# Making the scores of a whole group of heads in one piece, in eleven of sixteen groups

## The chip, the cores and the metric

The kernel runs on one core of a Trainium2 chip. The metric is the device time of one execution in microseconds (us), of which the median of several runs is taken. Engines are named as in the profile: PE is TensorE's matmul stream, DVE VectorE, ACT ScalarE, POOL GpSimd, SP the queue of SyncE.

## The reference, cut to what matters

```python
def attention(xn, ctx, mask, wq, wk, wv, wo):        # 32 sequences of 64 tokens, 512 wide
    q = rope((xn @ wq) in 32 heads of 128)
    k = rope((ctx @ wk) in 8 heads of 128, each used by 4 query heads)
    v = (ctx @ wv) in 8 heads of 128, likewise
    p = softmax(q @ k.T / sqrt(128) + mask)           # 64 x 64 per sequence and head
    return (p @ v) @ wo
x = x + tanh(g_xattn) * attention(layernorm(x), ctx, ctx, mask, ...)
x = x + tanh(g_ffn) * lora_top1_experts(layernorm(x))
```

Everything is float32. Most products are made as three products of split operands (high and low parts); the scores alone are float32 products without a split.

## The kernel before

**Stages.** Up to about 205 us the kernel makes the keys and values of all sequences. Then come 64 attention steps, `k = 0..63`, from about 216 us to the end; the last four (`WIDE = 60` and on) are written out by hand, together with the end of the experts. Four steps make a group of heads `G = k // 4`: one key head with its four query heads, over half of the sequences (16 of them, in two chunks of 8 sequences, each chunk in two steps of 4). Groups 0 to 7 are the first half of the sequences, groups 8 to 15 the second. In the first half the query weights (`weights_of`) and output weights are also split and stored beside the steps, until step 25; in the second half they are fetched ready.

**One step `k` on PE** (loop at L1065): the scores that are due; `times_values(k-1)`, probabilities times values, into the banks `attn[0]` and then `attn[1]`; two query products of the next group (each 6 matmuls, L892); `project_out(k-1, 0)` (12 matmuls, L963); in even steps a third product; `turn_probs(k)` (4 transposes, L923); `project_out(k-1, 1)`; and a last product (`last`). The query blocks are made by a seven-product scheme: blocks `b` of two heads, products numbered 0 to 6, and from them four sums `j` (`q_sum`, `SUMS`), each of which then gets its rotary embedding: DVE multiplies by the cosine (`q_cos`, L1197), ACT copies the halves crosswise (`q_shift`, L1605 and L1606), POOL multiplies by the sine (`by_sin`, L1885), DVE adds (`q_add`, L1202). Product 6, and the sum `j = 3` that needs it, end the making of a block.

**Scores.** `scores(k)` is 32 matmul instructions of 128 rows by 64 columns (L912) into bank `score` or `small`. Steps in `PAIRED` (2 to 29 and 36 to 59) make them two by two at the head of every even step, so a group has two such places. `scores` waits for the rotary adds of its queries, for its keys, and for `masked`, the mask add that last read its bank.

**Softmax of step k.** DVE adds the mask out of the bank (L1263) and finds the maximum (L1268), POOL subtracts (L1892), ACT takes the exponential (L1635), DVE sums and inverts (L1272, L1274), POOL multiplies (L1897), PE transposes, ACT copies the high part (`prob_high`, L1643, L1646), DVE makes the low part (`prob_low`, L1284).

**What PE waits for around the values.** `times_values(k)` needs both low parts of step k before its first matmul. Its second half, into `attn[1]`, also needs `x1_added` to have reached `2k`, which means that `add_out(k-1, 1)` (DVE, L1304) has read what `project_out(k-1, 1)` left in that bank:

```python
e.wait_ge(probs_low, 2 * k + 2)
...
e.wait_ge(x1_added, 2 * k - 1 + bp)
```

The order on every engine is written out by hand, and each engine runs its instructions in that order.

Of the kernel before, what the change touches and what calls it, by code (L numbers as in the profile page):

```python
# [36 lines left out]
UNITS = GROUPS * CHUNKS  # L37
# [4 lines left out]
SCALE = float(np.float32(1) / np.sqrt(np.float32(DH)))  # L42
SPLIT_PRODUCTS = ((0, 0), (0, 1), (1, 0))
TWIN_ROWS = (slice(0, SEQ), slice(SEQ, 2 * SEQ))

RAW = 2
WO_SLOTS = GROUP + 2
# [132 lines left out]
def ropes_of(k):  # L180

    early, late = sums_of(k)
    pending = sums_of(k - 1)[1] if k else [(1, 3)]
    pending = [q for q in pending if q[1] == 3]
    rest = [q for q in late if q[1] != 3]
    if len(early) == 2:
        return early[:1], early[1:], rest
    return pending, early, rest
# [116 lines left out]
def build(nc, x, ctx, mask, g_attn, g_ffn, wq, wk, wv, wo, routed_w, lora_b, table, out):  # L305
# [8 lines left out]
    with ExitStack() as stack:  # L314
# [263 lines left out]
        def _(e):  # L578
# [199 lines left out]
            for k in range(STEPS + 1):  # L778
                for j in range(k):
                    for n in wo_late(j) if wo_low_step(j) == k - 1 else ():  # L780
                        store_wo(n)
                done = KT + sum(len(wo_late(j)) for j in range(k) if wo_low_step(j) < k)
                while ring < min(len(RING), RAW + done):
                    fetch_raw(ring)
                    ring += 1
                for b, piece in weights_of(k):
                    if piece == 1 and k and b + 1 < HEAD_PAIRS_ALL:
                        fetch_wq_raw(b + 1)
                    if piece == 3:
                        store_wq(b)  # L790
                if k % 2 == 0 and HEAD_PAIRS_ALL <= k // 2 + 3 < Q_BLOCKS:
                    fetch_wq(k // 2 + 3)
                if k in (27, 28):
                    for i in {27: range(4), 28: range(4, BLOCKS)}[k]:
                        fetch_xB(i)
                if k % 2 == 1 and k // 2 + 2 < UNITS:
                    fetch_keys(k // 2 + 2)
                if k % 2 == 0 and k and k // 2 + 1 < UNITS:
                    fetch_values(k // 2 + 1)
                if k % 4 == 0:  # L800
                    G = k // 4
                    for n in range(max(GROUP * G + 2, HEADS), min(GROUP * G + 6, GROUP * GROUPS)):
                        fetch_wo(n)
                if k in (30, 32):
                    fetch_mask(CHUNKS + (k - 30) // 2)
                for t in range(HALF_TILES):
                    if 30 + t // 2 == k - 1:
                        store(t)
# [7 lines left out]
        def _(e):  # L816
# [248 lines left out]
            for k in range(1, WIDE):  # L1065
                first, middle, last = products_of(k)
                if k in PAIRED:
                    for j in (k, k + 1) if k % 2 == 0 else ():
                        scores(j)
                elif k > 1:  # L1070
                    scores(k)
                between(k, 0)
                times_values(k - 1)
                between(k, 1)
                for b, i in first[:1]:
                    product(b, i)
                between(k, 2)
                for b, i in first[1:]:
                    product(b, i)
                between(k, 3)  # L1080
                project_out(k - 1, 0)
                between(k, 4)
                for b, i in middle:
                    product(b, i)
                turn_probs(k)
                between(k, 5)
                project_out(k - 1, 1)
                between(k, 6)
                for b, i in last[:1]:
                    product(b, i)  # L1090
                between(k, 7)
                for b, i in last[1:]:
                    product(b, i)
                between(k, 8)

            k = WIDE
# [59 lines left out]
        def _(e):  # L1156
# [93 lines left out]
            def by_row(k):  # L1250
                return prob_of(k)[:, :].rearrange("p (r k) -> p r k", r=ROWS)

            def mask_scores(k, tiles=()):
                u, s = divmod(k, SUBS)
                G, c, index = chunk_of(u)
                m = mask_sb[:, c, s * SUB_SEQS:(s + 1) * SUB_SEQS, :].rearrange("p b k -> p (b k)").unsqueeze(1).to_broadcast(
                    [P, HEAD_PAIRS, SUB_SEQS * SEQ])
                e.wait_ge(scored, k + 1)
                e.wait_ge(mask_in[c], 16 * (index // CHUNKS + 1))
                if k >= 2:  # L1260
                    e.wait_ge(probs_turned, k - 1)
                by_head = prob_of(k)[:, :].rearrange("p (h n) -> p h n", h=HEAD_PAIRS)
                e.scalar_tensor_tensor(out=by_head, in0=scores_bank(k)[:, :].rearrange("p (h n) -> p h n", h=HEAD_PAIRS),  # L1263
                                       scalar=SCALE, in1=m, op0=ALU.mult, op1=ALU.add).then_inc(masked, 1)

                expert_norms_end(tiles)
                e.wait_ge(masked, k + 1)
                e.tensor_reduce(neg_max[:, k % 2, :], by_row(k), AX.X, ALU.max, negate=True).then_inc(max_found, 1)  # L1268

            def sum_rows(k):  # L1270
                e.wait_ge(exponentials, k + 1)
# [151 lines left out]
            for k in range(1, WIDE):  # L1423
                early, late = sums_of(k)
                ropes = ropes_of(k)
                mask_scores(k, norms_of(k - 1))
                attn_low(k - 1, 0)
                attn_low(k - 1, 1)
                between(k, 0)
                between(k, 1)  # L1430
                if k % 4 != 1 and k > 2:
# [4 lines left out]
                    for n in wo_late(k - 1):  # L1436
                        raw_low(("wo", n))

                for q in sums_of(k - 1)[1] + early:
                    q_sum(*q)  # L1440

                for q in (ropes_of(0)[0], ropes_of(1)[0])[k - 1] if k <= 2 else ():
                    q_cos(*q)
                    q_add(*q)
                if k > 2:
                    ropes_left(k - 1)
                between(k, 2)
                add_out(k - 1, 0)
# [9 lines left out]
                between(k, 5)  # L1458
                between(k, 6)
                prob_low(k, *((0, 1) if together else (1,)))  # L1460
                add_out(k - 1, 1)
                if k <= 2:
                    ropes_left(k - 1)
# [358 lines left out]
        def _(e):  # L1822
# [107 lines left out]
            for k in range(1, WIDE):  # L1930
                ropes = ropes_of(k)
                pieces = weights_of(k)
                subtract_max(k)
                if k == 1:
                    for q in ropes_of(0)[0]:
                        by_sin(ROPE_NO["q", *q])
                elif k == 2:
                    weight_low(*weights_of(1)[1])
                elif k % 2 == 0 and pieces:
                    combine_weights(pieces[0][0], (0,))  # L1940
                elif k % 4 == 1:
                    for n in wo_late(k - 1):
                        raw_low(("wo", n))
                elif pieces:
                    weight_low(*(pieces[0] if k > 3 else weights_of(2)[0]))
# [4 lines left out]
                if k == 1:  # L1950
# [2 lines left out]
                    for q in ropes_of(0)[1]:  # L1953
                        by_sin(ROPE_NO["q", *q])
                    combine_weights(HEAD_PAIRS + 1, (1,))
                if k % 2 == 0 and pieces:
                    combine_weights(pieces[0][0], (1,) if k > 2 else (0, 1))
                for q in ropes[0]:
                    by_sin(ROPE_NO["q", *q])
# [7 lines left out]
                    weight_low(*pieces[0 if k % 4 == 1 else 1])  # L1967
                if k % 2 == 0 and k > 2 and pieces:

                    e.wait_ge(rope_added, ROPE_NO["q", *ropes[0][0]] + 1)  # L1970
                    weight_low(*pieces[0])
                for q in ropes[1] + ropes[2]:
                    by_sin(ROPE_NO["q", *q])
# [80 lines left out]
```

## Time and profile before

| | us |
|---|---|
| median of 3 runs (1054.49 to 1057.78) | 1055.28 |
| time of the profiled execution | 1054.43 |
| its span | 1052.6 |
| PE busy | 1043.5 (99%) |
| DVE busy | 871.8 (83%) |
| ACT busy | 634.2 (60%) |
| POOL busy | 592.0 (56%) |

The profile comes from one execution. Busy times are of the span of 1052.6 us; its own run took 1.8 us more. Times in rows are us from the span's start. A merged row of the timeline gives the start of its first instruction, the time to the modelled end of the last, and the count. Matmuls overlap, so what a stretch of matmuls takes is read from its start to the start of the next row.

### The profile page before, as it was taken

The numbers are of one execution on the slowest core, as the hardware profiler recorded it, in microseconds if no ns is written. First come the engines' busy times: TensorE is split into PE (matmuls) and PEld (weight loads), VectorE is DVE, ScalarE is ACT, GpSimd is POOL, SyncE is SP. The second block draws the span as 40 slices with busy tenths as digits, with TensorE's granted clock in tenths as the row PEclk, the third lists the DMA queues.
The fourth block names the chain that finished last, engine by engine and source line by source line (L and its number), as shares of the span: only waits on it lengthen the run. The fifth ranks groups of instructions, "written<-read, shape, count | busy, mean of one in ns | idle before, by whom it ended". The sixth has DMA issues, their size and how long they took to land.

```text
span 1052.6 us, 19130 instructions
## 1 busy us (share of the span) xinstructions
PE 1043.5 (99%) x6664; PEld 865.2 (82%) x6664; DVE 871.8 (83%) x1423; ACT 634.2 (60%) x1112; POOL 592.0 (56%) x518
## 2 busy tenths in 40 slices
PE   9999999999999999999999999999999999999998
PEld 7888888877788888888888888888888888888786
DVE  7875766788888888888887999888788788888997
ACT  7554456676766676767666645555555555555653
POOL 4552379887878787878764433333443334444423
PEclk9999999999999999999999999999999999999999
DMA  7768966476765656566469745563546464644102
GB/s 262 269 226 302 395 232 240 160 282 211 249 219 182 218 183 208 192 191 210 150 246 398 247 150 171 160 198 119 201 124 201 127 197 121 194 121 134 46 26 81
DMA packets 106094, 206.40 MB, mean 196 GB/s; under 512 B 8848, under 2 KB 58640, under 8 KB 100112
## 3 DMA queue, kind: packets, MB, share of 16 engines
q1 hardware_dynamic: 105424, 204.40, 57.3%
q8 instruction: 55, 0.90, 0.4%
q10 hardware_dynamic: 576, 0.79, 0.2%
q14 instruction: 39, 0.32, 0.1%
HBM read 122.31 MB, written 82.84 MB: 195 GB/s over the span
## 4 chain that ended last, share of the span: by engine, by line
PE 91%; DVE 5%; POOL 2%; issue 1%; ACT 1%; DMA 0%; DVEq 0%; SPq 0%; ACTq 0%
PE attn L963 31%; PE proj L892 27%; PE attn L854 8%; PE score L854 4%; PE turned L854 4%; PE attn L948 3%; PE score L912 3%; PE turned L923 3%; PE attn L950 3%; PE small L912 2%; PE proj L826 1%; DVE acc L1304 1%; DVE stats L1162 1%; DVE o_s L1292 0%; DVE p_low L1284 0%
## 5 line engine op out<-in xcount | busy, mean ns | idle before, releaser
L963 PE MATMUL attn<-wo_s,o_s 128*128 128x512 f32 x1524 | 375.1, 395 | 0.6 <-DVE o_s L1292 0.5
L892 PE MATMUL proj<-xB,wq_s 128*128 128x512 f32 x1344 | 332.7, 390 | 0.0
L963 PEld LDWEIGHTS attn<-wo_s,o_s 128*128 128x128 f32 x1524 | 280.7, 188 | 58.3 <-DVE o_s L1292 1.4
L892 PEld LDWEIGHTS proj<-xB,wq_s 128*128 128x128 f32 x1344 | 251.8, 188 | 51.8 <-issue 0.4
L1885 POOL TENSOR_TENSOR rot<-rot,tab 128x512 f32<-128x512 f32 x110 | 163.3, 1485 | 146.7 <-ACT rot L1606 146.6
L1655 ACT ACTIVATE o_s<-attn 128x512 fp32r<-128x512 f32 x127 | 69.2, 596 | 89.0 <-PE attn L950 88.8
L1197 DVE TENSOR_TENSOR q_r<-q_r,tab 128x512 f32<-128x512 f32 x127 | 116.5, 918 | 1.5 <-ACT x_third L1606 1.4
L1292 DVE TENSOR_TENSOR o_s<-attn,o_s 128x512 fp32r<-128x512 f32 x127 | 81.9, 685 | 32.3 <-ACT o_s L1655 32.3
L1627 ACT ACTIVATE copies<-proj 128x512 f32<-128x512 f32 x96 | 57.5, 599 | 76.9 <-PE proj L892 76.6
L1304 DVE SCALAR_TENSOR_TENSOR acc<-attn,gates_t,acc 128x512 f32<-128x512 f32 x127 | 94.9, 748 | 6.8 <-PE attn L963 3.8
L1885 POOL TENSOR_TENSOR rot_third<-rot_third,tab 128x512 f32<-128x512 f32 x40 | 61.7, 1542 | 58.3 <-ACT rot_third L1606 55.4
L1284 DVE TENSOR_TENSOR p_low<-turned,p_high 64x512 fp32r<-64x512 f32 x128 | 87.8, 686 | 5.2 <-ACT p_high L1643 2.8
L1643 ACT ACTIVATE p_high<-turned 64x512 fp32r<-64x512 f32 x128 | 75.5, 590 | 26.2 <-PE turned L923 24.4
L1605 ACT ACTIVATE rot<-q_r 64x512 f32<-64x512 f32 x84 | 52.4, 623 | 53.1 <-DVE q_r L1241 51.3
L1646 ACT ACTIVATE p_high<-p_high 64x512 fp32r<-64x512 f32 x128 | 80.8, 631 | 2.8
L1241 DVE TENSOR_TENSOR q_r<-copies,proj 128x512 f32<-128x512 f32 x127 | 81.1, 678 | 0.3 <-PE proj L892 0.3
L1202 DVE TENSOR_TENSOR q_r<-q_r,rot 128x512 f32<-128x512 f32 x85 | 69.2, 814 | 6.0 <-POOL rot L1885 0.3
L1897 POOL TENSOR_TENSOR prob_even<-prob_even,row_inv 128x512 f32<-128x512 f32 x32 | 34.1, 1065 | 60.5 <-DVE row_inv L1274 60.5
L1897 POOL TENSOR_TENSOR prob_odd<-prob_odd,row_inv 128x512 f32<-128x512 f32 x32 | 35.8, 1117 | 39.1 <-DVE row_inv L1274 39.1
L948 PE MATMUL attn<-p_high,v_s 128*128 128x256 f32 x254 | 55.0, 298 | 2.1 <-issue 0.7
L1831 POOL TENSOR_TENSOR rstd<-var_eps,power 128x1 f32<-128x1 f32 x32 | 18.5, 578 | 68.1 <-DVE var_eps L1166 68.1
L1892 POOL TENSOR_TENSOR prob_even<-prob_even,neg_max 128x512 f32<-128x512 f32 x32 | 33.4, 1044 | 38.8 <-DVE neg_max L1268 38.8
(272 smaller groups left out, 1733.4 us busy)
## 6 DMA issues: line engine op xcount, KB each, us to landing
wq_kept<-wq_s SPq DMA_DIRECT2D x16, 1792.0 KB, 6.3
wq_s<-wq_kept SPq DMA_DIRECT2D x16, 1792.0 KB, 8.8
v_kept<-vst SPq DMA_DIRECT2D x64, 256.0 KB, 4.3
v_s<-v_kept SPq DMA_DIRECT2D x128, 128.0 KB, 4.8
wo_kept<-wo_s SPq DMA_DIRECT2D x32, 512.0 KB, 6.0
wo_s<-wo_kept SPq DMA_DIRECT2D x32, 512.0 KB, 5.4
k_kept<-kst SPq DMA_DIRECT2D x32, 256.0 KB, 2.1
wq_raw<-in_wq SPq DMA_DIRECT2D x16, 512.0 KB, 7.7
```

What stands on the lines that cost most here:

```text
L854: last = e.matmul(b[:, :], stationary, moving, start=(kt == 0 and m == 0), stop=(kt == KT - 1 and m == 2))
L892: last = e.matmul(dst[:, :], wq_s[:, b % 2, A, s, kt, :], xB[:, B, mv, kt, :], start=(first and kt == 0 and m == 0), stop=(kt == 1 and m = ...
L948: e.matmul(b[:, cols[twin]], v_s[:, u % 2, twin, tiles[bp], :], p_high[:, twin, cols[bp]], start=(twin == 0), stop=False, skip_group_check ...
L963: last = e.matmul(out_bank(k, bp)[:, :], o_s[:, s, bp, h, :], wo_s[n % WO_SLOTS][:, m, :], start=(h == 0 and i == 0), stop=(h == GROUP - 1 ...
L1197: e.tensor_tensor(dst, src, cos, ALU.mult).then_inc(times_cos, 1)
L1241: e.tensor_tensor(q_tile(b, j) if dst is None else dst, by_seq(copies[:, copy, :]), by_seq(proj[PRODUCTS[i][2]][:, :]), ALU.add).then_inc( ...
L1284: e.tensor_tensor(p_low[rows, :, twin, :], turned[rows, :].rearrange("p (b n) -> p b n", b=PAIRS), p_high[rows, twin, :].bitcast(F32).rear ...
L1292: e.tensor_tensor(low, src, high.bitcast(F32), ALU.subtract).then_inc(out_low, 1)
L1304: e.scalar_tensor_tensor(out=acc[:, tile, :], in0=out_bank(k, bp)[:, :], scalar=gates_t[:, 0:1], in1=acc[:, tile, :], op0=ALU.mult, op1=AL ...
L1643: e.activation(p_high[rows, twin, :], turned[rows, :], ACT.Copy).then_inc(probs_high, 1)
L1646: last = e.activation(p_high[TWIN_ROWS[1 - twin], twin, :], p_high[rows, twin, :].bitcast(F32), ACT.Copy)
L1885: e.tensor_tensor(r3, r3, sin, ALU.mult).then_inc(times_sin, 1)
```

## The change

`QUADS` names eleven groups, 2 to 6 and 9 to 14. In them all four `scores` of the group are made at its first step, behind query products 0 and 1 and ahead of `project_out(k-1, 0)`; the pair at the head of the group's first step and the one at the head of its third step go. Since the last two of the four need the queries of the second chunk, product 6 of the last step of the group before is made ahead of `project_out(k-1, 1)` instead of behind it, its sum and the cosine of sum 2 go ahead of `add_out(k-1, 1)` on DVE, and the remaining rotary work goes to the head of the first step. DVE adds the masks of two steps there (`add_mask`) and finds their maxima apart (`find_max`). On POOL the combining of weights goes ahead of the first step's subtraction; on SP the keys are fetched in other steps. The diff:

```diff
+QUADS = (*range(2, 7), *range(9, 15))
+def in_quad(k):
+    return k // 4 in QUADS
+def quad_begins(k):
+    return k % 4 == 0 and in_quad(k)
...
@@ ropes_of
-    pending = [q for q in pending if q[1] == 3]
-    rest = [q for q in late if q[1] != 3]
+    pending = [q for q in pending if q[1] == 3 and not quad_begins(k)]
+    rest = [q for q in late if q[1] != 3 or quad_begins(k + 1)]
...
@@ SP
-                if k % 2 == 1 and k // 2 + 2 < UNITS:
+                if k % 4 == 2 and quad_begins(k + 2):
+                    fetch_keys(k // 2 + 2)
+                elif k % 2 == 1 and k // 2 + 2 < UNITS and not quad_begins(k + 1):
                     fetch_keys(k // 2 + 2)
...
@@ PE
-                    for j in (k, k + 1) if k % 2 == 0 else ():
+                    for j in (k, k + 1) if k % 2 == 0 and not in_quad(k) else ():
                         scores(j)
...
                 for b, i in first[1:]:
                     product(b, i)
+                if quad_begins(k):
+                    for j in range(k, k + 4):
+                        scores(j)
                 between(k, 3)
                 project_out(k - 1, 0)
...
                 turn_probs(k)
                 between(k, 5)
+                for b, i in last[:1] if quad_begins(k + 1) else ():
+                    product(b, i)
                 project_out(k - 1, 1)
                 between(k, 6)
-                for b, i in last[:1]:
+                for b, i in last[:1] if not quad_begins(k + 1) else ():
                     product(b, i)
...
@@ DVE (mask_scores is split into add_mask and find_max)
-                mask_scores(k, norms_of(k - 1))
-                attn_low(k - 1, 0)
-                attn_low(k - 1, 1)
+                if quad_begins(k):
+                    second, third = ropes_of(k - 1)[1] + ropes_of(k - 1)[2]
+                    q_add(*second)
+                    q_cos(*third)
+                    attn_low(k - 1, 0)
+                    q_add(*third)
+                    add_mask(k)
+                    add_mask(k + 1)
+                    find_max(k)
+                    attn_low(k - 1, 1)
+                else:
+                    if k % 4 == 1 and in_quad(k):
+                        find_max(k)
+                    else:
+                        mask_scores(k, norms_of(k - 1))
+                    attn_low(k - 1, 0)
+                    attn_low(k - 1, 1)
...
-                for q in sums_of(k - 1)[1] + early:
+                for q in early if quad_begins(k) else sums_of(k - 1)[1] + early:
                     q_sum(*q)
...
-                if k > 2:
+                if k > 2 and not quad_begins(k):
                     ropes_left(k - 1)
...
                 prob_low(k, *((0, 1) if together else (1,)))
+                if quad_begins(k + 1):
+                    q_sum(*late[0])
+                    q_cos(*ropes[1][0])
                 add_out(k - 1, 1)
...
@@ POOL
+                if quad_begins(k) and pieces:
+                    combine_weights(pieces[0][0])
                 subtract_max(k)
...
                 elif k % 2 == 0 and pieces:
-                    combine_weights(pieces[0][0], (0,))
+                    if not quad_begins(k):
+                        combine_weights(pieces[0][0], (0,))
...
-                if k % 2 == 0 and pieces:
+                if k % 2 == 0 and pieces and not quad_begins(k):
                     combine_weights(pieces[0][0], (1,) if k > 2 else (0, 1))
...
-                    e.wait_ge(rope_added, ROPE_NO["q", *ropes[0][0]] + 1)
+                    if ropes[0]:
+                        e.wait_ge(rope_added, ROPE_NO["q", *ropes[0][0]] + 1)
```

## Rows read from the trace of the kernel before

**Rows 1.** Busy time by stretch: PE, PEld, DVE, ACT, POOL, granted clock, DMA share, GB/s

```profile
306.99:561.99 255.00, 255.00 (x1741) 212.51 (x1740) 225.08 (x328) 174.47 (x307) 195.36 (x168) 1.00 0.62 210
683.34:989.34 306.00, 306.00 (x2090) 255.01 (x2089) 247.59 (x384) 175.56 (x300) 124.07 (x97) 1.00 0.48 149
```

**Rows 2.** The list of waits, PE on DVE's output add: total, times, longest

```profile
PE attn L948 <- DVE acc L1304: 0.5, 1, 0.5
```

**Rows 3.** PE's timeline, step 23 and the head of step 24: start, us, instruction

```profile
499.95 0.40 PE L948 MATMUL attn<-p_high,v_s 128*128 128x256 f32 x2
...
500.41 0.40 PE L948 MATMUL attn<-p_high,v_s 128*128 128x256 f32 x2
...
500.89 2.90 PE L892 MATMUL proj<-xB,wq_s 128*128 128x512 f32 x12
503.63 2.88 PE L963 MATMUL attn<-wo_s,o_s 128*128 128x512 f32 x12
...
509.54 1.52 PE L892 MATMUL proj<-xB,wq_s 128*128 128x512 f32 x6
510.99 1.15 PE L912 MATMUL score<-k_r,q_r 128*64 128x64 f32 x32
...
513.01 0.50 PE L948 MATMUL attn<-p_high,v_s 128*128 128x256 f32 x2
...
513.58 0.40 PE L948 MATMUL attn<-p_high,v_s 128*128 128x256 f32 x2
```

**Rows 4.** Timeline at the kernel's end: scores alone, and a wait for the output add

```profile
989.34 1.15 PE L912 MATMUL score<-k_r,q_r 128*64 128x64 f32 x32
990.42 0.50 PE L948 MATMUL attn<-p_high,v_s 128*128 128x256 f32 x2
...
1002.05 0.50 PE L948 MATMUL attn<-p_high,v_s 128*128 128x256 f32 x2 [0.55 <-DVE acc L1304]
```
```profile
1001.25 0.75 DVE L1304 SCALAR_TENSOR_TENSOR acc<-attn,gates_t,acc 128x512 f32<-128x512 f32 x1
```

**Rows 5.** DVE's timeline, head and end of step 23 (first half)

```profile
499.38 0.75 DVE L1304 SCALAR_TENSOR_TENSOR acc<-attn,gates_t,acc 128x512 f32<-128x512 f32 x1
...
508.96 1.60 DVE L1202 TENSOR_TENSOR q_r<-q_r,rot 128x512 f32<-128x512 f32 x1
510.48 1.40 DVE L1284 TENSOR_TENSOR p_low<-turned,p_high 64x512 fp32r<-64x512 f32 x2
511.91 0.75 DVE L1304 SCALAR_TENSOR_TENSOR acc<-attn,gates_t,acc 128x512 f32<-128x512 f32 x1
```

**Rows 6.** The page's groups of DVE: cosine products and query sums

```profile
L1197 DVE TENSOR_TENSOR q_r<-q_r,tab 128x512 f32<-128x512 f32 x127 | 116.5, 918 | 1.5 <-ACT x_third L1606 1.4
...
L1241 DVE TENSOR_TENSOR q_r<-copies,proj 128x512 f32<-128x512 f32 x127 | 81.1, 678 | 0.3 <-PE proj L892 0.3
```

**Rows 7.** The timelines of DVE and PE, end of step 21 (first half)

```profile
485.66 0.69 DVE L1284 TENSOR_TENSOR p_low<-turned,p_high 64x512 fp32r<-64x512 f32 x1
486.39 0.75 DVE L1304 SCALAR_TENSOR_TENSOR acc<-attn,gates_t,acc 128x512 f32<-128x512 f32 x1
```
```profile
487.51 0.50 PE L948 MATMUL attn<-p_high,v_s 128*128 128x256 f32 x2
```

**Rows 8.** The timelines of PE, DVE, ACT and POOL, step 47 (second half)

```profile
825.29 0.40 PE L948 MATMUL attn<-p_high,v_s 128*128 128x256 f32 x2
...
831.70 0.60 PE L923 MATMUL turned<-tab,prob_odd 128*128 128x128 f32 x4
```
```profile
831.90 0.75 DVE L1304 SCALAR_TENSOR_TENSOR acc<-attn,gates_t,acc 128x512 f32<-128x512 f32 x1 [0.22 <-PE attn L963]
...
834.08 1.40 DVE L1284 TENSOR_TENSOR p_low<-turned,p_high 64x512 fp32r<-64x512 f32 x2
```
```profile
835.38 0.63 ACT L1606 ACTIVATE rot_third<-q_r 64x512 f32<-64x512 f32 x1
```
```profile
836.09 1.27 POOL L1885 TENSOR_TENSOR rot_third<-rot_third,tab 128x512 f32<-128x512 f32 x1 [3.27 <-ACT rot_third L1606]
```

More of the change, by code:

```diff
@@ L1251, in by_row, with add_mask @@
                 return prob_of(k)[:, :].rearrange("p (r k) -> p r k", r=ROWS)
-            def mask_scores(k, tiles=()):
+            def add_mask(k):
                 u, s = divmod(k, SUBS)
@@ L1264, in mask_scores, with find_max @@
                                        scalar=SCALE, in1=m, op0=ALU.mult, op1=ALU.add).then_inc(masked, 1)
-                expert_norms_end(tiles)
+            def find_max(k):
                 e.wait_ge(masked, k + 1)
                 e.tensor_reduce(neg_max[:, k % 2, :], by_row(k), AX.X, ALU.max, negate=True).then_inc(max_found, 1)
+            def mask_scores(k, tiles=()):
+                add_mask(k)
+                expert_norms_end(tiles)
+                find_max(k)
             def sum_rows(k):
@@ L1425, in _ @@
                 ropes = ropes_of(k)
-                mask_scores(k, norms_of(k - 1))
-                attn_low(k - 1, 0)
-                attn_low(k - 1, 1)
+                if quad_begins(k):
[4 more added lines that the diff above has]
+                    q_add(*third)
+                    add_mask(k)
+                    add_mask(k + 1)
[3 more added lines that the diff above has]
+                    if k % 4 == 1 and in_quad(k):
+                        find_max(k)
+                    else:
+                        mask_scores(k, norms_of(k - 1))
+                    attn_low(k - 1, 0)
+                    attn_low(k - 1, 1)
                 between(k, 0)
```

## The prediction, made before the changed kernel had run

> **What bounds the kernel now.** I read the busy times by stretch first, then PE's list of waits, then the timelines of single steps. In both halves of the attention PE is busy for every microsecond of the stretch at full clock, and DVE for 225 of 255 us in the first half but 248 of 306 in the second [rows 1]. PE's waits are nearly nothing, and only once, at the kernel's end, does it wait for the output add [rows 2]. So the order in which PE issues matmuls sets the time, and what can be gained is only what PE itself loses between them. What can be lost is slack: how long before PE needs something the other engines have it. The first-half steps must be read apart from the second-half ones, since DVE (88% busy against 81%) has less room there.
>
> **What goes: eleven entries into the scores.** The cost of one is read around the pair ahead of step 24 [rows 3]. Going in: the six matmuls of a product take 1.45 us up to the scores (509.54 to 510.99), where twelve undisturbed ones take 2.74 (500.89 to 503.63), so six take 1.37: 0.08 lost. Inside: 64 score instructions take 2.02 us (510.99 to 513.01), and 32 alone take 1.08 (989.34 to 990.42) [rows 4], so 32 more cost 0.94 and a place costs 1.08 - 0.94 = 0.14 beyond its instructions. Going out: the first half of the values takes 0.57 us (513.01 to 513.58) against 0.46 (499.95 to 500.41): 0.11. Sum 0.33; with the times unrounded I take 0.35. The eleven changed groups have two places each and get one. The new place is left into `project_out`, which the trace shows no dearer, so the gain is 11 x 0.35 = **3.9 us**. The bound from below is 11 x 0.25 if leaving into wider matmuls costs another 0.1. No matmul is added or dropped.
>
> **What is added (1): the turn of the group.** Product 6 (1.37 us) changes places with `project_out(k-1, 1)`, and the pair of scores (2.02) goes from behind it. These 3.4 us lay between `project_out(k-1, 1)` and `times_values(k)`, and were the cover for `add_out(k-1, 1)`. Now the values follow at once, and their second half needs that add. The trace lets me time every part. PE's last `project_out` matmul is followed at 831.70 by the transposes and DVE's add begins at 831.90: 0.20 us [rows 8]. The add takes 0.75, and PE goes on 0.05 after it (1002.00 to 1002.05) [rows 4]. The first half of the values covers 0.46 [rows 3]. So PE must stop for 0.20 + 0.75 + 0.05 - 0.46 = **0.54 us** at each of eleven turns, even if DVE is idle. This alone is 5.9 us against the gain of 3.9.
>
> DVE is not idle. Ahead of the add the change queues a `q_sum` (0.60 of pitch, its 0.68 [rows 6] less the 0.08 by which such instructions overlap) and a `q_cos`. In the second half the low parts end at 835.48 and a sum would end by 836.1; the `q_cos` waits for ACT's shift, as late now as before, which ends 10.72 into the step (836.01 - 825.29) [rows 8]. A `q_cos` that meets no POOL work takes 0.69, the mean of all is 0.92 [rows 6]. With 0.69 the add runs from 11.36 to 12.11 and PE's second half starts at 12.16. A step without scores is 510.99 - 499.95 = 11.04, less the 0.08 of going in: 10.96 [rows 3], so it would have started at 11.42. The stop is **0.74** at each of the six second-half turns: 4.4 us.
>
> In the first half the low parts of step 23 end at 511.88, which is 11.93 into the step, and DVE had run without a break before them (the add of the sine part ends at 510.56, the low parts start at 510.48) [rows 5]. Sum, cosine and add behind them take 0.60 + 0.60 + 0.67: the add ends at 13.80, PE's second half starts at 13.85 instead of 11.42: a stop of 2.4 us at the turn into group 2. At the four later turns PE has already come 0.6 us closer to DVE (next part) while DVE itself gains 0.3, so I take 2.65. Five turns: 2.4 + 4 x 2.65 = **13.0 us**.
>
> **What is added (2): the middle of the group.** At step 4G+2 the pair of scores vanishes ahead of `times_values(4G+1)`, and with it 2.02 + 0.08 = 2.10 us of cover. In the first half the low part of step 21 ends at 486.35, 1.16 before the values start at 487.51, and the add at 487.14, 0.83 before the second half at 487.97 to 488.08 [rows 7]. The values would start at 485.41 and their second half at 485.87; the add is ready for PE at 487.19. Stop: **1.3 us**, five times: 6.6. The change takes one mask add from DVE in that step, but DVE stands idle there anyway before it waits for ACT, so I credit nothing. In the next step DVE's slack is 0.28 (add ends at 500.13 [rows 5], second half starts at 500.41 [rows 3]) and PE is 0.9 ahead of its old time, DVE 0.35: a stop of 0.35, four times: 1.4. In the second half the low parts of the corresponding steps are ready some 3 us ahead, and 2.1 less does not hurt: step 47 as the nearest case has them at 10.19 of 10.96 [rows 8]. Nothing.
>
> **What is added (3): four scores in a row.** The third shares its bank with the first, so it waits for `add_mask(k)`. That has 0.20 + 0.69 + 0.05 = 0.94 us and the second scores take 0.94 [rows 4]; I take 0.05 at each place, 0.5 in all, and 0 to 0.2 as the bounds. It also waits for the rotary add of sum 3. In the second half its shift ends about 12.1, the sine product about 14, the add about 15.5 into the count above, and the third scores would start at 17.6. In the first half PE's own stop gives that chain more time. It is covered; every microsecond by which it were later than 2 us would cost 11. The softmax of the first step has 6.9 us from the second scores' end to the transposes, and needs about 6.1 (two DVE passes and the small inverse, two on POOL at 1.04, one on ACT); 0.8 is left. If that cover went, each 0.1 costs 1.1. Edits with one answer: the weight combining moves into POOL time that is free while PE makes scores; SP's key fetches wait for scores that are made earlier than before, and come at least one step ahead of use. Both at nothing; a late key fetch would stop PE by the lateness.
>
> **The sum.** Stops 4.4 + 13.0 + 6.6 + 1.4 + 0.5 = 25.9, gain 3.9: **+22.0 us**. The profiled execution took 1054.43, of which 1.8 lie around the span and stay: 1076.4. The median of the runs is 0.85 above it, so I forecast **1077** for the median. For the spread I let each first-half stop be off by a quarter (5 us) and `q_cos` take its mean: 1069 to 1084.
>
> **Rivals.** (a) *DVE catches up.* The work that leaves the later steps lets DVE reach the values in time in the first half, and only the eleven turns stop PE. For it: DVE has 30 us of idle time per 255 in the first half [rows 1]. Against it: its idle time lies ahead of what it waits for from ACT, not in the run before the low parts. Price: 11 x 0.74 + 0.5 - 3.9 = +4.7, 1060.
> (b) *Faster.* The turn is hidden too, and the place's cost is all that counts: 1055.28 - 3.9 = 1051. This decides where the stop at a turn is under 0.35 us; the bound of 0.54 is above that, so the bound would have to be wrong, for example if the wait for `add_out` fell on work that had ended.
> (c) *POOL takes the turn from DVE.* `q_cos(2)` on DVE and the sine product of the same sum on POOL are both released by one ACT shift. POOL's product takes 1.27 us alone, starting 0.08 after the shift [rows 8]. If it holds DVE off, the cosine ends about 1.2 later, and so do add and values: up to 11 x 1.2 = 13 more, 1090. Against it: DVE starts 0.03 to 0.05 after ACT, POOL 0.08. The Trainium skill (SBUF — State Buffer, "SBUF: two separate sides") says that the two share a port pair as an exclusive lock, and whoever starts first holds it for the whole instruction; by that rule this case is all or nothing, decided by those few hundredths. The 0.81 to 1.12 us that some cosine products take beside POOL speak for such holding off.
> (d) *Not what it says.* The third scores wait on queries that come late, so the four fall into two pieces; it costs what the chain is late, and I count it with (c).
>
> **How the numbers follow.** Forecast 0.70, (a) 0.12, (b) 0.04, (c) and (d) 0.14. The range takes in the forecast's own spread and reaches towards (a) and (c): 1065 to 1086. A difference of 0.3% (3.2 us) is what a measurement of this kernel tells from none. Faster by more is (b) alone: 0.04. Within it lies half of (a) with small turns: 0.08. Slower: 0.88.
>
> **What would show it.** After the change PE's list of waits should have about 11 entries of the second half of the values (L948) behind DVE's output add (L1304), 0.7 us each in the second half and 2 to 3 us in the first, and five to nine entries in the middle of first-half groups. The score places should fall by eleven, each at 3.9 us. The prediction is wrong if PE stays as full in the first half as now, if DVE's add at a turn ends within 0.8 us of `project_out`, or if the stops lie at the scores or at the transposes instead.

## The result and the profile after

The changed kernel takes 1095.31 us (median of 4 runs, 1091.34 to 1096.69) against 1055.31: a ratio of 1.0366, 95% interval 1.0338 to 1.0395. It is 40 us slower; the forecast was 22 us slower, with a range that ended at 1086. The profiled execution took 1096.69 us, 42.3 more than the one of before, and this is what the accounts below are made against. One execution of the kernel before (1994 us, granted clock 0.88) and one of the kernel with filled stops (1515 us, 0.66) ran in a slow state and are left out of every median and ratio below.

PE's list of waits in the changed kernel (total, times, longest). L962 is the first matmul of each half of `times_values`, L948 before; L1328 is DVE's output add, L1304 before. Before, the second line of this list read 0.5 us, once [rows 2]:

```profile
PE attn L962 <- DVE acc L1328: 17.2, 12, 1.8
PE attn L962 <- issue: 9.9, 11, 1.1
...
PE proj L906 <- issue: 0.6, 1, 0.6
```

The eleven turns and the middles of first-half groups are there, as forecast. The first line is the second half of the values, at the eleven turns and once at the kernel's end. The second is the low parts, at the five first-half turns, in the five first-half middles, and once ahead of the changed groups. What is not in this list is in the table of stretches (busy time of PE, PEld, DVE, ACT, POOL, granted clock, DMA share, GB/s), the turn into group 2 and one of the second half:

```profile
310.00:315.00 5.00, 4.27 (x13) 3.46 (x14) 4.65 (x6) 3.02 (x6) 4.21 (x3) 0.66 0.34 143
820.00:825.00 5.00, 5.00 (x49) 3.90 (x50) 1.62 (x3) 0.83 (x2) 0.00 (x0) 0.71 0.56 163
```

The granted clock (the value ahead of the DMA share) is 0.66 and 0.71: TensorE ran for part of these stretches at 1.2 instead of 2.4 GHz. Before, it was 1.00 in every stretch [rows 1].

**A second-half turn**, step 47 into 48, the timeline of PE, then of DVE, ACT and POOL. The same places before are in [rows 8]:

```profile
868.35 2.88 PE L977 MATMUL attn<-wo_s,o_s 128*128 128x512 f32 x12
871.07 0.40 PE L962 MATMUL attn<-p_high,v_s 128*128 128x256 f32 x2
871.30 0.39 PE L964 MATMUL attn<-p_low,v_both 128*128 128x512 f32 x1
873.46 0.50 PE L962 MATMUL attn<-p_high,v_s 128*128 128x256 f32 x2 [1.76 <-DVE acc L1328]
873.80 0.39 PE L964 MATMUL attn<-p_low,v_both 128*128 128x512 f32 x1
874.03 2.92 PE L906 MATMUL proj<-xB,wq_s 128*128 128x512 f32 x12
876.88 1.15 PE L926 MATMUL score<-k_r,q_r 128*64 128x64 f32 x32
877.86 1.10 PE L926 MATMUL small<-k_r,q_r 128*64 128x64 f32 x32
879.02 1.15 PE L926 MATMUL score<-k_r,q_r 128*64 128x64 f32 x32
...
881.04 1.20 PE L977 MATMUL attn<-wo_s,o_s 128*128 128x512 f32 x4
```
```profile
868.90 1.40 DVE L1308 TENSOR_TENSOR p_low<-turned,p_high 64x512 fp32r<-64x512 f32 x2
870.34 0.69 DVE L1260 TENSOR_TENSOR q_r<-copies,proj 128x512 f32<-128x512 f32 x1
870.95 1.79 DVE L1216 TENSOR_TENSOR q_r<-q_r,tab 128x512 f32<-128x512 f32 x1
872.66 0.74 DVE L1328 SCALAR_TENSOR_TENSOR acc<-attn,gates_t,acc 128x512 f32<-128x512 f32 x1
...
878.08 0.69 DVE L1282 SCALAR_TENSOR_TENSOR prob_even<-score,mask_sb 128x512 f32<-128x512 f32 x1 [1.85 <-PE score L926]
```
```profile
870.20 0.63 ACT L1647 ACTIVATE rot_third<-q_r 64x512 f32<-64x512 f32 x1
```
```profile
870.91 1.28 POOL L1926 TENSOR_TENSOR rot_third<-rot_third,tab 128x512 f32<-128x512 f32 x1 [3.27 <-ACT rot_third L1647]
```

The second half of the values would have started at 871.07 + 0.46 = 871.53 and starts at 873.46: a stop of 1.92 us (the row's 1.76 counts from the modelled end of the matmul ahead). The cosine took 1.79 us where 0.69 was forecast. POOL's sine product had started at 870.91, 0.04 before it, and took its own 1.28. Five of the six second-half turns are like this (POOL ahead by 0.02 to 0.04, cosine 1.79 to 1.81); at the first POOL is ahead by 0.41, the cosine takes 1.42 and the stop is 1.90. The four scores take 881.04 - 876.88 = 4.16 us: the third begins 1.16 after the second, where 0.93 is the pace. After the stop PE starts 0.11 slower (0.34 instead of 0.23 for the first pair of matmuls).

**A first-half turn**, step 19 into 20, timelines of PE and DVE:

```profile
474.09 2.88 PE L977 MATMUL attn<-wo_s,o_s 128*128 128x512 f32 x12
478.05 0.47 PE L962 MATMUL attn<-p_high,v_s 128*128 128x256 f32 x2 [1.07 <-issue]
...
479.98 0.50 PE L962 MATMUL attn<-p_high,v_s 128*128 128x256 f32 x2 [1.23 <-DVE acc L1328]
```
```profile
476.55 1.40 DVE L1308 TENSOR_TENSOR p_low<-turned,p_high 64x512 fp32r<-64x512 f32 x2
477.97 0.69 DVE L1260 TENSOR_TENSOR q_r<-copies,proj 128x512 f32<-128x512 f32 x1
478.58 0.69 DVE L1216 TENSOR_TENSOR q_r<-q_r,tab 128x512 f32<-128x512 f32 x1
479.18 0.74 DVE L1328 SCALAR_TENSOR_TENSOR acc<-attn,gates_t,acc 128x512 f32<-128x512 f32 x1
```

`project_out` ends at 474.09 + 2.72 = 476.81, PE stops 1.23 us for the low parts and, 0.46 after it goes on, 1.47 more for the add: 2.70. "Issue" stands at the first stop because the profile names no releaser; the low parts end at 477.95 and PE starts 0.10 later. The cosine takes 0.69: POOL's product of 476.65 ended at 477.92, and its next starts at 480.04.

**A first-half middle**, step 18, PE's timeline:

```profile
450.52 1.52 PE L906 MATMUL proj<-xB,wq_s 128*128 128x512 f32 x6
452.82 0.47 PE L962 MATMUL attn<-p_high,v_s 128*128 128x256 f32 x2 [0.78 <-issue]
...
453.56 0.51 PE L962 MATMUL attn<-p_high,v_s 128*128 128x256 f32 x2
```

The six matmuls would be done at 450.52 + 1.37 = 451.89, so PE stops 0.93 for the low parts. The second half starts 0.74 after the first instead of 0.46. Together that is 1.21.

### The profile page after: what moved, and what is told of

It is laid out like the page before. It is cut to its first block, busy times and chain, and to the rows that moved or that the text cites. A ratio compares the mean times of both kernels' runs of the same rounds, so it can differ in the third digit from the quotient of the medians.

```text
span 1094.9 us, 19125 instructions
## 1 busy us (share of the span) xinstructions
PE 1058.1 (97%) x6664; PEld 871.0 (80%) x6664; DVE 875.8 (80%) x1423; ACT 636.9 (58%) x1112; POOL 592.3 (54%) x518
## 4 chain that ended last, share of the span: by engine, by line
PE 61%; DVE 16%; POOL 9%; issue 7%; SPq 3%; ACT 2%; DMA 2%; DVEq 0%; ACTq 0%; POOLq 0%
PE attn L977 23%; PE proj L906 21%; DVE q_r L1216 4%; PE score L926 3%; PE attn L962 2%; PE small L926 2%; PE turned L937 2%; DVE acc L1328 2%; POOL wq_s L1901 2%; POOL rot L1926 2%; PE attn L964 2%; PE attn L868 2%; DVE p_low L1308 2%; DVE q_r L1260 1%; PE score L868 1%
## 5 line engine op out<-in xcount | busy, mean ns | idle before, releaser
L906 PE MATMUL proj<-xB,wq_s 128*128 128x512 f32 x1344 | 341.6, 398 | 0.8 <-issue 0.6
L906 PEld LDWEIGHTS proj<-xB,wq_s 128*128 128x128 f32 x1344 | 256.6, 192 | 54.4 <-issue 1.6
L1926 POOL TENSOR_TENSOR rot<-rot,tab 128x512 f32<-128x512 f32 x110 | 160.7, 1461 | 172.9 <-ACT rot L1647 172.7
L1216 DVE TENSOR_TENSOR q_r<-q_r,tab 128x512 f32<-128x512 f32 x127 | 120.7, 950 | 1.5 <-ACT x_third L1647 1.4
L1328 DVE SCALAR_TENSOR_TENSOR acc<-attn,gates_t,acc 128x512 f32<-128x512 f32 x127 | 94.9, 748 | 18.1 <-PE attn L977 16.3
L962 PE MATMUL attn<-p_high,v_s 128*128 128x256 f32 x254 | 55.8, 301 | 28.2 <-DVE acc L1328 17.2
L962 PEld LDWEIGHTS attn<-p_high,v_s 128*128 128x128 f32 x254 | 43.8, 188 | 46.2 <-DVE acc L1328 24.6
L1221 DVE TENSOR_TENSOR q_r<-q_r,rot 128x512 f32<-128x512 f32 x85 | 71.7, 844 | 5.3 <-POOL rot L1926 0.3
L1676 ACT ACTIVATE prob_even<-prob_even 128x512 f32<-128x512 f32 x32 | 20.2, 630 | 68.8 <-POOL prob_even L1933 68.8
```

The source lines that it names most:

```text
L906: last = e.matmul(dst[:, :], wq_s[:, b % 2, A, s, kt, :], xB[:, B, mv, kt, :], start=(first and kt == 0 and m == 0), stop=(kt == 1 and m = ...
L962: e.matmul(b[:, cols[twin]], v_s[:, u % 2, twin, tiles[bp], :], p_high[:, twin, cols[bp]], start=(twin == 0), stop=False, skip_group_check ...
L1216: e.tensor_tensor(dst, src, cos, ALU.mult).then_inc(times_cos, 1)
L1221: e.tensor_tensor(dst, src, by_seq(rotated(r)), ALU.add).then_inc(rope_added, 1)
L1328: e.scalar_tensor_tensor(out=acc[:, tile, :], in0=out_bank(k, bp)[:, :], scalar=gates_t[:, 0:1], in1=acc[:, tile, :], op0=ALU.mult, op1=AL ...
L1926: e.tensor_tensor(r3, r3, sin, ALU.mult).then_inc(times_sin, 1)
```

## The experiments

Two questions: where do the stops at the turns come from, and what makes up the 20 us that the forecast lacks? My theory of them was the one of the prediction (lost cover) with its rival (c) for the second half, and the clock for the rest. Each time is given with that of before on the same chip.

### Only the second half

```diff
-QUADS = (*range(2, 7), *range(9, 15))
+QUADS = (*range(9, 15),)
```

> The scores are grouped in groups 9 to 14 only; groups 2 to 6 are as before. The trace of the changed kernel has the scores at 588.9 and 562.0 before at the end of the first half, 26 us more than at its start, and 15 more in the second half. If both halves cost for themselves: +15 us over before (six turns of 1.95 and one or two stretches at the lower clock of 1.7), that is 1070, and a first half as full as before. If the first half's delay carries over into the second: less than 10.

1070.4 us (1067.63 and 1073.16) against 1054.74, ratio 1.0148 (1.0085 to 1.0210). The first half is as full as before:

```profile
307.00:562.00 255.00, 255.00 (x1741) 212.53 (x1740) 225.04 (x328) 174.50 (x307) 195.62 (x168) 1.00 0.61 210
```

So each half pays for itself. The two runs differ by 5.5 us, and so do their clocks (0.998 and 0.994 over the span, a difference worth 4.3 us).

### The output add ahead of sum and cosine

```diff
-                if quad_begins(k + 1):
-                    q_sum(*late[0])
-                    q_cos(*ropes[1][0])
                 add_out(k - 1, 1)
+                if quad_begins(k + 1):
+                    q_sum(*late[0])
+                    q_cos(*ropes[1][0])
```

> Changed kernel, but DVE's output add of the turn runs ahead of the sum and the cosine. Theory that the add's place behind the cosine is what costs in the second half: PE's stop at a second-half turn falls from 1.92 us to the bare 0.54 (0.20 + 0.75 + 0.05 - 0.46), eight tenths of what is lost there; at a first-half turn the second stop falls from 1.4 to about 0.1, since the add then follows the low parts at once. Sum 6 x 1.4 + 5 x 1.3 = 15 us less than the changed kernel, 1080. Rival, that the add waits for PE's project_out and not for its queue: no change, 1095.

1079.07 us (1078.33 and 1079.82) against 1054.74, ratio 1.0230 (1.0200 to 1.0260). PE's timeline at the same turn:

```profile
858.45 0.40 PE L962 MATMUL attn<-p_high,v_s 128*128 128x256 f32 x2
...
859.46 0.51 PE L962 MATMUL attn<-p_high,v_s 128*128 128x256 f32 x2 [0.38 <-DVE acc L1328]
```

859.46 - 858.45 - 0.46 = 0.55 us, the bare stop of the prediction, at all six turns. A second-half group takes 51.55 instead of 52.95 us, as expected. The time is 1 us from what was expected, but that is luck, for two things were not foreseen. In the first half the third scores now wait 0.8 us longer, since the masks stand behind rotary work that comes later (4.4 us over five times in the list of waits), so a first-half group takes 55.0 instead of 55.33 and gives back 0.3 of the 1.3 us that were expected. And the clock is 1.00 in both runs, which gives back what the changed kernel loses by it (0.992 to 0.997 over its span), some 6 us at the median.

### The same two instructions in the other order

```diff
-                    q_sum(*late[0])
                     q_cos(*ropes[1][0])
+                    q_sum(*late[0])
```

> Changed kernel, but DVE's cosine of sum 2 ahead of its sum 3 at the turn: same two instructions, other order. Both the cosine and POOL's sine product are released by the same ACT shift. Theory that one holds the other off and that the first to start wins: the cosine now starts 0.03 to 0.05 us after ACT, ahead of POOL's 0.08, so in the second half it takes 0.7 instead of 1.79 us, POOL's product takes 1.7 instead of 1.28, and the stop falls from 1.92 to about 1.3 us: 4 us less in all, 1091. Rival, that only the length of the queue counts: the stop stays at 1.92 or grows by the 0.4 us that DVE now waits for the shift.

1090.51 us (1089.34 and 1091.69) against 1054.74, ratio 1.0338 (1.0308 to 1.0368). The timelines of DVE, POOL and PE at the turn into step 48:

```profile
866.51 0.69 DVE L1216 TENSOR_TENSOR q_r<-q_r,tab 128x512 f32<-128x512 f32 x1 [0.57 <-ACT rot_third L1647]
867.24 0.69 DVE L1260 TENSOR_TENSOR q_r<-copies,proj 128x512 f32<-128x512 f32 x1
867.84 0.75 DVE L1328 SCALAR_TENSOR_TENSOR acc<-attn,gates_t,acc 128x512 f32<-128x512 f32 x1
```
```profile
866.56 1.77 POOL L1926 TENSOR_TENSOR rot_third<-rot_third,tab 128x512 f32<-128x512 f32 x1 [3.28 <-ACT rot_third L1647]
```
```profile
866.72 0.40 PE L962 MATMUL attn<-p_high,v_s 128*128 128x256 f32 x2
...
868.64 0.50 PE L962 MATMUL attn<-p_high,v_s 128*128 128x256 f32 x2 [1.30 <-DVE acc L1328]
```

DVE starts 0.05 us ahead of POOL, its cosine takes 0.69 instead of 1.79, and POOL's product 1.77 instead of 1.28, at all six second-half turns. The stop falls from 1.92 to 868.64 - 866.72 - 0.46 = 1.46 (1.3 was expected) although DVE waits for the shift, which it did not do in the changed kernel. So it is who starts first that decides, which settles rival (c). The whole time is no proof of it: the second half gives back 6 x 0.46 = 2.8 us, each first-half turn costs 0.12 more, and the rest of the 4.8 us, 2.6, goes with the higher clock (0.996 and 0.995). The Trainium skill (SBUF — State Buffer, "SBUF: two separate sides") has the port pair of the two as an exclusive lock for the whole instruction; these two traces agree, with 0.49 to 1.10 us as the price for the one that comes second. They agree nearly, not wholly: the cosine that came second ended 0.55 us after POOL's product and POOL's product 1.13 after the cosine, each 0.14 to 0.15 less than it takes alone.

### The scores in pairs again, all else as changed

```diff
-                    for j in (k, k + 1) if k % 2 == 0 and not in_quad(k) else ():
+                    for j in (k, k + 1) if k % 2 == 0 else ():
                         scores(j)
...
-                if quad_begins(k):
-                    for j in range(k, k + 4):
-                        scores(j)
```

> The changed order of product 6, sum 3, cosine and rotary work at the turn, but the scores stay in pairs at the heads of the even steps. Theory that the scores were the cover: the pair gives 2.1 us back at each turn and in the middle of each group. Second half: stop 1.92 - 2.1, so none, and the time of a group is 51.0 as before. First half: middle 0, turn 2.5 - 2.1 = 0.4 us, five times: +2 us over before, 1057. Rival, that the new order of the other engines is what costs: over 1075.

1084.94 us (1083.76 and 1086.13) against 1054.74, ratio 1.0285 (1.0256 to 1.0315): missed by 28 us. PE's waits:

```profile
PE turned L937 <- POOL prob_even L1935: 20.3, 12, 3.0
PE attn L962 <- DVE acc L1325: 1.5, 6, 0.6
```

The theory held at the values: 1.5 us are left of 17.2 there, so the pair is the cover. But a new stop stands at the transposes of each group's first step, 3.0 us in the first half and 0.75 to 0.9 in the second. In the changed order DVE does the masks and the maximum behind two rotary adds, a cosine and `attn_low`. At the first step of group 2 the first mask starts at 314.01, where the pair of scores begins at 307.20 and ends before 309.21: this softmax starts late, and has no piece of scores behind it. The clock falls here too (0.995 and 0.993). The expectation forgot that the new order of DVE is made for scores that come 3.7 us later. It says nothing against the theory of the cover, and shows that the new order of the other engines can't stand without the four scores.

### The second pair of scores back in the middle of the group

```diff
-                    for j in (k, k + 1) if k % 2 == 0 and not in_quad(k) else ():
+                    for j in (k, k + 1) if k % 2 == 0 and not quad_begins(k) else ():
...
-                    for j in range(k, k + 4):
+                    for j in range(k, k + 2):
```

> The changed kernel, but the scores of a group's last two steps are made in a pair at the head of its third step again, so only the first two stand behind the query products. Theory that in the first half the middle of the group costs 1.7 us (1.2 at the values of the odd step, 0.3 at those of the next, 0.2 for starting again) because the pair of 2.1 us was its cover: a first-half group falls from 55.3 to 53.7 us, with 0.3 more gone for the mask wait between the second and third scores, less 0.35 for the second place. A second-half group, which has no stop there, stays at 53.0. Together 1095 - 8 = 1087. Rival, that DVE is late in the first half whatever stands there: 55.3 stays.

1096.67 us (1095.69 and 1097.64) against 1055.25, ratio 1.0391 (1.0372 to 1.0410): missed by 10 us, though its clock (0.998 and 0.997) is no lower than the changed kernel's best (0.997). Its waits:

```profile
PE attn L962 <- DVE acc L1328: 17.3, 12, 1.8
PE turned L937 <- POOL prob_even L1938: 11.1, 12, 1.0
PE attn L962 <- issue: 5.5, 6, 0.9
```

The stops in the middle of first-half groups are gone: the line "issue" falls from 9.9 us in 11 places to 5.5 in 6. In their place PE waits 1.1 us for the transposes of the first step, in all eleven groups. The third and fourth scores were the cover of the first step's softmax. The 2.15 us that they take ahead of `project_out` less 1.1 leave 1.05 us of slack in the changed kernel; the prediction had counted 0.8 and found nothing late, rightly. A first-half group takes 54.86 us where 53.7 was expected, and a second-half group 54.2 where 53.0 was.

### The stops filled

`fill` issues matmuls into a bank that the next product overwrites; nothing reads them.

```diff
+                if turn_here and k < HALF_STEPS:
+                    fill(products_of(k + 1)[0][0][0], 5)
                 e.wait_ge(v_in[u % 2], 80 * (u // 2 + 1))
...
                 for bp in pairs:
+                    if turn_here and bp == 1:
+                        fill(products_of(k + 1)[0][0][0], 6 if k < HALF_STEPS else 8)
```

> The changed kernel with matmuls that nothing reads, put where PE stops at a turn: in the first half 5 ahead of the values and 6 between their two halves, in the second half 8 between the halves, each 0.23 us, so no longer than the stops (1.2, 1.4 and 1.9 us). Its output is the reference's. Theory that the stretches at the lower clock (five of 3.41 us in the changed kernel's trace, each worth 1.65 us, all begun within 3 us of a turn's stop) come from PE standing still: the granted clock is 1.00 at every turn and the time falls by up to 8 us, 1087 to 1090. Rival, that the scores in one piece or something else brings the clock down: clock 0.99 and 1095 as before.

1089.17 us (median of three, 1088.59 to 1090.36) against 1055.25, ratio 1.0322 (1.0306 to 1.0338). The same two stretches, and PE's timeline at the turn into step 48:

```profile
310.00:315.00 5.00, 5.00 (x44) 3.83 (x44) 4.84 (x6) 3.19 (x6) 4.04 (x3) 1.00 0.42 181
820.00:825.00 5.00, 5.00 (x77) 4.41 (x78) 3.28 (x7) 0.63 (x1) 2.04 (x2) 1.00 0.16 45
```
```profile
864.95 0.40 PE L977 MATMUL attn<-p_high,v_s 128*128 128x256 f32 x2
...
867.36 0.51 PE L977 MATMUL attn<-p_high,v_s 128*128 128x256 f32 x2
```

The stops are as long as they were (the second half of the values starts 2.41 us after the first at the turn into step 48, 867.36 against 864.95, where it was 2.39), but PE works in them, and the granted clock is 1.00 here and over the whole span, in all three executions. A second-half group takes 53.0 us, always; in the changed kernel it takes 52.95, or 54.6 where the clock falls. So the lower clock comes from PE standing still at the turn, and not from the scores in one piece, which are the same in both. The changed kernel's trace has five such falls, each 3.41 us long and beginning 0.2 to 0.9 us after the values' second half has started at a turn; they cost 1.65 each: 8.2 us. Its runs have from two to five of them by their mean clocks (0.997 to 0.992), and this is their spread of 5 us.

### Product 6 behind project_out

In all eleven groups; DVE's output add goes ahead of sum 3 and the cosine, as above.

```diff
-                for b, i in last[:1] if quad_begins(k + 1) else ():
-                    product(b, i)
                 project_out(k - 1, 1)
                 between(k, 6)
-                for b, i in last[:1] if not quad_begins(k + 1) else ():
+                for b, i in last[:1]:
                     product(b, i)
```

> All eleven groups make their scores in one piece, but product 6 of the turn stays behind project_out, and DVE's output add goes ahead of sum 3 and the cosine. Theory that the turn's cover is this product: in the second half no stop is left at the turn, a group takes 51.0 - 0.35 + 0.28 (the wait of the third scores for the mask) = 50.9 us. In the first half the low parts are late by 1.0 us at the turn and 1.4 to 1.7 in the middle stay, and the third scores wait about 1 us for late queries: 54.5 us. Together 1055 + 5 x 3.5 = 1072. Rival, that the scores' place itself is what costs in the second half: a group stays above 52.

1077.44 us (1076.84 and 1078.03) against 1055.25, ratio 1.0209 (1.0190 to 1.0227), 5 us above what was expected. No second-half turn stops at the values any more. A second-half group takes 51.3 us, 0.4 more than expected, because the third scores now wait for the last rotary add and the masks behind it (PE's timeline):

```profile
862.67 1.15 PE L926 MATMUL score<-k_r,q_r 128*64 128x64 f32 x32
863.65 1.10 PE L926 MATMUL small<-k_r,q_r 128*64 128x64 f32 x32
865.16 1.15 PE L926 MATMUL score<-k_r,q_r 128*64 128x64 f32 x32 [0.41 <-DVE prob_even L1280]
```

1.51 from the second to the third instead of 0.93. A first-half group takes 55.0, 0.5 more than expected: as in the kernel with the add first, the low parts at turn and middle stay late. The two together are the 5 us. The clock is 1.00 in both runs.

### A third bank, in the second half only

Groups 9 to 14, product 6 behind, add first, and

```diff
+def scores_place(k):
+    if in_quad(k):
+        return ("small", "turned", "score", "small")[k % 4]
+    return "small" if k in PAIRED and k % 2 == 1 else "score"
...
-            return small if scores_in_small(k) else score
+            return {"small": small, "turned": turned, "score": score}[scores_place(k)]
```

> Groups 9 to 14 only, product 6 behind project_out, DVE's output add first, and the scores of the group's second step in the bank of the transposed probabilities, which is free at that time, so that the third scores wait for nobody. Theory: no stop is left and the bare gain of a place shows, 0.35 us for each of six groups: a second-half group takes 50.65 us, together 1055.3 - 2.1 = 1053.2, a ratio of 0.998. Rival, that scores in one piece gain nothing or wait elsewhere (rotary work of the second chunk, transposes): 51.0 or more, ratio 1.000 or above.

1052.73 us (median of 11 runs) against 1055.25 (14 runs), ratio **0.9978**, interval 0.9968 to 0.9987: 2.3 us faster than before by the ratio, 42.6 faster than the changed kernel, and 17.7 faster than the same six groups in the order of the change. PE's timeline at the head of a second-half group:

```profile
786.29 2.90 PE L913 MATMUL proj<-xB,wq_s 128*128 128x512 f32 x12
789.12 1.15 PE L933 MATMUL small<-k_r,q_r 128*64 128x64 f32 x32
790.11 1.10 PE L933 MATMUL turned<-k_r,q_r 128*64 128x64 f32 x32
791.04 1.10 PE L933 MATMUL score<-k_r,q_r 128*64 128x64 f32 x32
791.97 1.10 PE L933 MATMUL small<-k_r,q_r 128*64 128x64 f32 x32
793.01 3.02 PE L986 MATMUL attn<-wo_s,o_s 128*128 128x512 f32 x12
```

Nothing stops: 0.93 from bank to bank, 3.89 us for the four. From one such place to the next are 50.68 us where two pairs make 51.0 (306.00 for six groups, [rows 1]). The difference, 0.32, is the gain of one entry less that the prediction had worked out as 0.33 to 0.35 from the rows of before. Six of them make 1.9 of the 2.3 us; the interval of the ratio is 1.4 to 3.4.

## Why the prediction was right in sign and short in size

**What held.** The gain per place (0.32 us in the last experiment). The bare stop at a turn: 0.54 forecast, 0.55 measured with the add first, so slower was certain as soon as product and scores had gone from behind `project_out`. The first half, stop by stop: middle 1.3 forecast and 1.21 measured, next step 0.35 and 0.23, turn 2.65 and 2.70 (2.4 and 2.55 for the first). Their sum was 21.0 and came out at 20.3. That rival (a), DVE catching up, would not happen: its reason, idle time that lies ahead of ACT's work, is confirmed by stops that did not shrink. The softmax of the first step kept its slack. POOL's moved combining cost nothing that PE saw.

**What was mis-sized.** The table adds up what separates the two profiled executions, 42.3 us apart:

| term | forecast | measured |
|---|---|---|
| first-half turns, middles and steps behind them | 21.0 | 20.3 |
| second-half turns | 6 x 0.74 = 4.4 | 6 x 1.92 = 11.5 |
| third scores waiting for the mask | 0.5 | 11 x 0.28 = 3.1 |
| PE starting again: six second-half turns, and turn, middle and next step of the first half (5 + 5 + 4) | 0 | 20 x 0.11 = 2.2 |
| lower clock | 0 | 5 x 1.65 = 8.2 |
| products at step 28 | 0 | 0.7 |
| start of the attention | 0 | 0.7 |
| gain of eleven places (measured with the third bank) | -3.9 | 11 x 0.32 = -3.5 |
| sum | 22.0 | 43.2 |

The measured terms come out 0.9 us above the 42.3: for a second-half group they give 52.99 us and for a first-half group 55.43, where the trace has 52.95 and 55.33.

(1) *The second-half turn.* The step that failed is "with 0.69 the add runs from 11.36". It let the sum overlap the low parts by 0.08 and `q_cos` overlap the sum by as much, so that the cosine begins 10.75 into the step, just ahead of POOL at 10.80. But the sum starts 0.03 after the low parts instead of overlapping them: 10.22, not 10.11. So it ends at 10.91, and the cosine begins at 10.83, 0.03 to 0.04 behind POOL. The rows of before had the clue: an add behind low parts starts 0.03 to 0.04 after their end (511.88 to 511.91 in [rows 5], 486.35 to 486.39 in [rows 7]). Rival (c), which had 0.14 with (d), was the case in the second half at its full price of 1.18 us for six turns (at the first of them POOL was ahead by 0.41, with much the same stop), and not in the first half. The argument against it ("DVE starts 0.03 to 0.05 after ACT") forgot that DVE was not waiting for ACT but busy. It also quoted 0.81 to 1.12 us for cosines beside POOL, where the trace of before has some of 1.26 and one of 1.76. An outcome that hangs on 0.04 us, as at five turns, should have had a chance near one half.

(2) *The clock.* No part of the sum had it, and none of the rivals. All rows of before showed 1.00 [rows 1], with PE always busy; the forecast itself put stops of 1 to 3 us into that stream and never asked what the clock does then. It is the largest missing term, 8.2 of some 21 us, and it is in part chance: executions of the same kernel lose from two to five times 1.65.

(3) *The mask wait.* The step was "0.20 + 0.69 + 0.05 = 0.94". DVE's mask runs 878.08 to 878.77, as forecast, but PE's third scores start 0.25 after it, not 0.05. The 0.05 was read from the values after an add, another kind of matmul. The four scores take 4.16 with the wait and 3.89 with the third bank, which removes it.

(4) *Small ones.* PE's slower start after a stop was in the rows for entering and leaving scores, and was not applied to the new stops. At step 28 a product waits 0.7 us in the changed kernel, with the refetch of `xB` issued shortly before. The kernel that changes only the second half has no such wait. That the lighter step 26 takes the transfer's cover is my reading; no run isolates it. The attention starts 0.7 us later in this execution (first values at 217.16 instead of 216.41), ahead of anything that was changed; that is scatter between executions, for with the pair in the middle, which has the same changes at this place, they start at 216.37.

Of the rivals, (b) was excluded by the bound that it named, (d) did not occur in the changed kernel: its third scores wait for the mask only.

## What to carry to other kernels

Work that an engine does between writing a bank and using it again is cover for whoever empties it, so before moving it, write down the return path (latency, the emptying instruction, latency) and take off what stays. If the rest is positive, a stop is certain whatever else is true. On a bound engine price a stop with what comes along: the slower start and the clock. And give an instruction that leaves one queue at the same moment as a rival on another both of its durations.

## What the runs showed of the hardware

A DVE product of two SBUF operands and a POOL product shut each other out for nearly a whole instruction: with POOL 0.04 us ahead, DVE's took 1.79 instead of 0.69 us; with DVE 0.05 ahead, POOL's took 1.77 instead of 1.28.

TensorE's granted clock fell from 2.4 to 1.2 GHz for 3.41 us at a time at five of eleven turns, after PE had stood still for 1.9 us (or 1.1 to 1.2 and 1.5 in a row). With the scores in pairs it was 0.52 on average from 320 to 327 us, about a stop of 3.0 us that ended at 320.70. It did not fall when matmuls that nobody reads filled those stops, nor in either execution of the kernel with the add first, whose longest stops were 1.2 us (granted clock 1.00). The same work can have it or not from one execution to the next, which is why the changed kernel's runs spread over 5 us. Of the 21 runs of the kernel before, 18 lie within 1.4 us and three some 1.4 to 2 us above those, two of them with a recorded clock of 1.00; what lengthened them stays open.

A float32 score matmul that waits for DVE starts 0.25 us after the instruction that it waits for; the split matmuls of the values start 0.05 to 0.06 after an output add and 0.10 after the low parts.
